# Mixing stage of a four-layer model: whole k and r products, state multiplies on GpSimd, another order of the steps

## The chip, the cores and the metric

The kernel runs on one core of a Trainium2 chip. A core has TensorE (matrix products), VectorE and ScalarE (elementwise work and activations), GpSimd (elementwise work as well) and SyncE, whose queue issues most DMA transfers. On-chip memory has 128 partitions; matrix products land in eight banks of a second memory, each 128 x 512 float32. Time is device microseconds of one execution, and lower is better.

## The reference

The model has four layers, each an attention-like part plus an expert part on a layer-normed input of 4 x 1024 tokens by 128 features. The change is in the first part of the last layer, and the last layer's 64 small experts run in the same stage.

```python
shifted = pad(x, one token)[:, :T];  delta = shifted - x
low = tanh((x + delta * mu_x) @ W_x1).reshape(B, T, 5, 32)
mus = einsum('blnr,dnr->blnd', low, W_x2) + x_bias
xr, xw, xk, xv, xg = [x + delta * mus[:, :, i] for i in range(5)]
r, k = xr @ W_r, xk @ W_k                      # 16 heads x 4
w = -exp(tanh(xw @ W_w1) @ W_w2 + b_w2)        # 16 heads x 4
v = xv @ W_v;  g = xg @ W_g                    # 16 heads x 8
def step(S, (r_t, k_t, v_t, w_t)):             # S: 4 x 8 per head
    o_t = r_t . S + (r_t * u * k_t).sum() * v_t
    S = exp(w_t) * S + outer(k_t, v_t)
o = group_norm(o) * gn_w + gn_b, times g * sigmoid(g), then @ W_o

# beside it: 64 experts and a shared one, 64 wide, top 8 of the router
out = sum_e gate_e * (silu(x @ Wg_e) * (x @ Wu_e)) @ Wd_e
```

## The kernel before

Everything lies transposed: features on the 128 partitions, the 4096 tokens along the row, cut into 8 chunks of 512 (`CH`, `BANK`). The last stage is `mixing_and_experts` (line 1739). It is written as a list of slots. From slot 12 on each slot holds one expert step: two experts, one chunk of tokens; 264 steps in all, 11 units of weights of 24 steps. The step goes through the engines with fixed lags. In slot t TensorE computes the hidden and the upper product (three float16 products each, from a high and a low part); ScalarE does silu in slot t; VectorE multiplies by the gate (`acted`, line 2298) and by the upper product (`scaled`, line 2304) in slot t+1; ScalarE makes the float16 high part in slot t+2 (line 2146); GpSimd makes the low part (`lows`, line 2185) in slot t+3; TensorE's output product stands in slot t+4. Every third step the sum is full: VectorE adds it to the result (line 2208) and TensorE may begin the next sum, in one bank, only after that.

The mixing lies between the steps. A chunk of it takes 33 slots (`PERIOD`), and the tables `PE_AT`, `ACT_AT`, `DVE_AT` and `POOL_AT` say in which slot of the chunk an engine does which job; a job of slot 37 falls into slot 4 of the next chunk. On each engine the order is: the expert step's work of the slot, then the mixing jobs, then on TensorE the output product. All waits are on counters of jobs done, so an engine that waits holds all that is queued behind it.

- TensorE's mixing products are float32 of 512 columns and take turns in two banks, `work`. A product waits until the reader of the last but one before it is done (`wait_bank`).
- Low-rank mixing factors: `low`, `low5`, `mu0` to `mu4`, then `mixed` (VectorE) and `x0` to `x4` (GpSimd) make the five inputs. `tanh_w`, `w` and two Exp on ScalarE (`ew`, `decay`) make the decay of 64 key rows, in `keys`. The Exp and the Sqrt each need a table load, and silu another one behind them.
- SyncE writes `keys` to DRAM (slot 10) and reads them back (slot 11) so that each row stands on the 8 partitions of its head's values: `rep`, 4 groups, one for each of a head's 4 keys. This read is called the spread here. SyncE also loads the gate rows, 6 transfers of 256 KB for every six steps into one of two buffers (line 1914), issued when the buffer's last reader is done, and the weights of the next unit (0.59 MB, line 1932).
- The state: for each group j TensorE computes the spread k (`k0` to `k3`) and r (`r0` to `r3`) with weights that repeat the columns; VectorE does `kv` (k times v), the `scan` along the tokens, `u` (adds u times kv to the state) and `rs` (times r); TensorE sums the four groups into `o_ps` (`o0` to `o3`), with the group mean taken off. Then `sq`, `var`, `std` (Sqrt), `rstd`, `norm`, `affine`, `gated`, and the product `out`, which VectorE adds to the result (`res`).

```python
banked = [job for job in pe_no if job[0] not in ("o0", "o1", "o2", "o3")]
bank_of = {job: i % 2 for i, job in enumerate(banked)}
bank_user = {job: banked[i - 2] for i, job in enumerate(banked) if i >= 2}
```

## Time and profile before

| | us |
|---|---|
| median of 3 runs | 4496.72 (4495.04 to 4506.08) |
| profiled execution | 4475.59 |
| its span, first to last instruction | 4473.8 |
| TensorE busy in the span | 3975.3 (89%) |
| VectorE busy | 3385.5 (76%) |
| ScalarE busy | 2913.3 (65%) |
| GpSimd busy | 2240.4 (50%) |

The expert steps of the last stage begin at 3744 us of the span. The shares of the table are means over all stages; for the change only the last one counts. A matmul's end in the trace is modelled: in a row of matmuls the starts tell the pace.

### The profile page before, as it was taken

Reading aid. Unit: us, or ns where it says so; the run is one execution under the profiler, and the core shown is the slowest. Engines: PE = TensorE matmul, PEld = TensorE weight load, DVE = VectorE, ACT = ScalarE, POOL = GpSimd, SP = SyncE. Lnnn points to the kernel's source line nnn. Section 1 sums busy time; section 2 is a strip of 40 time slices with the busy share of each in tenths; the row PEclk is TensorE's granted clock in tenths of the full one; section 3 lists DMA queues with packets and bytes.
Section 4 is the critical chain, followed back from the end, with each engine's and each line's share of the span. In section 5 each row is a group of like instructions: output and inputs, shape, how many; then the busy total and the mean of one; then the engine's idle time right before and its main releaser. Section 6 shows DMA issues by size and latency. Waiting matters only on the chain. (4 is left out here: it accounts for less than half of the span.)

```text
span 4473.8 us, 88017 instructions
## 1 busy us (share of the span) xinstructions
PE 3975.3 (89%) x34586; PEld 2227.3 (50%) x34588; DVE 3385.5 (76%) x4741; ACT 2913.3 (65%) x4403; POOL 2240.4 (50%) x1443
## 2 busy tenths in 40 slices
PE   6999999999999979996877777899788877999999
PEld 3666667666666654442111211245677543444443
DVE  6888888888884547767898899565877657878887
ACT  3777777777776449982677777685556644555555
POOL 2888888888886013331121210172566554555555
PEclk7999999999999989996899999898899988999999
DMA  3212212212210011100121100142000224454544
GB/s 84 59 40 59 58 38 59 59 40 58 58 35 16 1 49 48 71 24 29 50 74 43 40 27 16 57 149 72 11 13 15 75 83 115 113 124 116 120 113 108
DMA packets 113913, 270.28 MB, mean 60 GB/s; under 512 B 24276, under 2 KB 36308, under 8 KB 111004
## 3 DMA queue, kind: packets, MB, share of 16 engines
q1 hardware_dynamic: 98084, 223.86, 18.7%
q0 software_dynamic: 15424, 40.89, 2.6%
q8 instruction: 270, 4.42, 0.4%
q14 instruction: 135, 1.11, 0.1%
HBM read 178.10 MB, written 50.81 MB: 51 GB/s over the span
## 5 line engine op out<-in xcount | busy, mean ns | idle before, releaser
L522 POOL TENSOR_TENSOR a_prob_low<-a_prob_whole,a_prob_high 128x1024 f16<-128x1024 f32 x512 | 1085.0, 2131 | 276.7 <-ACT a_prob_high L412 275.6
L496 DVE TENSOR_REDUCE a_part_max<-a_top 128x2 f32<-128x1024 f32 x512 | 626.2, 1223 | 218.7 <-PE a_top L323 212.6
L409 ACT ACTIVATE a_prob_whole<-a_score 128x1024 f32<-128x1024 f32 x512 | 525.2, 1026 | 332.5 <-PE a_score L312 320.5
L976 ACT ACTIVATE a_prob<-a_score 128x512 f32<-128x512 f32 x1024 | 533.1, 603 | 255.9 <-PE a_score L915 255.8
L1009 DVE TENSOR_REDUCE a_part_max<-a_side 128x2 f32<-128x1024 f32 x512 | 595.2, 1220 | 68.3 <-PE a_side L886 68.3
L412 ACT ACTIVATE a_prob_high<-a_score 128x1024 f16<-128x1024 f32 x512 | 521.8, 1019 | 0.0
L311 PE MATMUL a_score<-a_qa,a_ka 128*128 128x256 f16 x2048 | 476.8, 273 | 0.0
L312 PE MATMUL a_score<-a_qb,a_kb 128*128 128x256 f16 x2048 | 476.5, 273 | 0.0
L2185 POOL TENSOR_TENSOR m_lows<-m_scaled,m_high 128x512 f16<-128x512 f32 x264 | 311.2, 1183 | 323.8 <-ACT m_high L2146 322.2
L378 PE MATMUL a_o_ps<-a_v,a_prob_high 128*128 128x65 f16 x4096 | 428.2, 193 | 6.2 <-POOL a_prob_low L522 3.4
L380 PE MATMUL a_o_ps<-a_v,a_prob_high 128*128 128x64 f16 x4096 | 427.0, 194 | 0.0
L382 PE MATMUL a_o_ps<-a_v,a_prob_low 128*128 128x65 f16 x4096 | 424.6, 192 | 0.0
L378 PEld LDWEIGHTS a_o_ps<-a_v,a_prob_high 128*128 128x128 f16 x4096 | 376.0, 96 | 85.7 <-DVE a_tokens L482 35.3
L380 PEld LDWEIGHTS a_o_ps<-a_v,a_prob_high 128*128 128x128 f16 x4096 | 377.8, 97 | 26.9 <-issue 10.9
L382 PEld LDWEIGHTS a_o_ps<-a_v,a_prob_low 128*128 128x128 f16 x4096 | 378.0, 98 | 0.0
L2138 ACT ACTIVATE m_up_down<-m_up_down 128x512 f32<-128x512 f32 x264 | 153.9, 583 | 341.4 <-PE m_up_down L1975 341.0
L915 PE MATMUL a_score<-a_qa,a_ka 32*128 32x512 f16 x1024 | 238.1, 399 | 90.6 <-ACT a_prob L976 88.0
L927 PE MATMUL a_o_ps<-a_prob,a_v 128*32 128x512 f32 x2048 | 287.6, 636 | 13.8 <-ACT a_raw L963 13.7
L915 PEld LDWEIGHTS a_score<-a_qa,a_ka 32*128 32x128 f16 x1024 | 60.4, 92 | 432.3 <-ACT a_prob L976 367.4
L2521 DVE TENSOR_TENSOR e_low<-e_whole,e_high 128x512 f16<-128x512 f32 x256 | 211.0, 834 | 83.9 <-ACT e_high L2479 82.9
L886 PE MATMUL a_side<-a_ka,a_qa 32*128 32x512 f16 x1024 | 218.1, 402 | 40.1 <-DVE a_part_max L1009 32.3
L2298 DVE TENSOR_TENSOR m_acted<-m_up_down,m_gate 128x512 f32<-128x512 f32 x264 | 180.4, 683 | 95.3 <-ACT m_up_down L2138 89.6
(477 smaller groups left out, 10147.8 us busy)
## 6 DMA issues: line engine op xcount, KB each, us to landing
m_gate<-gates SPq DMA_DIRECT2D x264, 256.0 KB, 5.2
a_ka<-a_nat_high_k SPq DMA_DIRECT2D x128, 128.0 KB, 2.4
e_gate<-gates SPq DMA_DIRECT2D x8, 2048.0 KB, 7.2
slots<-in_slots SPq DMA_DIRECT2D x19, 520.0 KB, 4.2
a_qa<-a_nat_high_q SPq DMA_DIRECT2D x64, 128.0 KB, 2.4
a_qa<-a_nat_low_q SPq DMA_DIRECT2D x64, 128.0 KB, 2.4
a_qb<-a_nat_high_q SPq DMA_DIRECT2D x64, 128.0 KB, 2.4
a_kb<-a_nat_low_k SPq DMA_DIRECT2D x64, 128.0 KB, 2.4
```

Source lines behind the costliest of these rows:

```text
L311: eng.matmul(score[:, e % 2, h, i, :], ka[:, r, h, keys], qa[:, r, h, qs], start=True, stop=False)
L312: mm = eng.matmul(score[:, e % 2, h, i, :], kb[:, r, h, keys], qb[:, r, h, qs], start=False, stop=True)
L378: eng.matmul(o_ps[:, at:at + V1], high, v[:, r, kt, h, 0:V1], start=(pair == 0 and i == 0 and h == 0 and t == 0), stop=False, skip_group_c ...
L380: eng.matmul(o_ps[:, at:at + DH], high, v[:, r, kt, h, V1 + 1:VW], start=False, stop=False, skip_group_check=True)
L382: mm = eng.matmul(o_ps[:, at:at + V1], low, v[:, r, kt, h, 0:V1], start=False, stop=last, skip_group_check=True)
L409: eng.activation(prob_whole[:, e % RING, :, :, :], score[:, e % 2, :, :, :], ACT.Exp, scale=scale)
L412: eng.activation(prob_high[:, e % RING, :, :, :], score[:, e % 2, :, :, :], ACT.Exp, scale=scale).then_inc(exp_done, 1)
L496: eng.tensor_reduce(part_max[:, i, c, :, qt % 4], top[:, :, :], AX.X, ALU.max).then_inc(max_done, 1)
L522: eng.tensor_tensor(prob_low[:, e % RING, :, :, :], prob_whole[:, e % RING, :, :, :], prob_high[:, e % RING, :, :, :], ALU.subtract).then_ ...
L976: eng.activation(prob[:, e % RING, h, :], score[:, step % SLOTS, :], ACT.Exp).then_inc(exp_done, 1)
L1009: op = eng.tensor_reduce(part_max[:, qt // 4, c, 2 * pair:2 * pair + 2, 24 + qt], side, AX.X, ALU.max)
L2185: eng.tensor_tensor(lows[:, s % HR, :], scaled[:, s % SR, :], high[:, s % HR, :], ALU.subtract).then_inc(low_done, 1)
```

## The change

The products for k and r are computed once for the 64 keys (`w_k` and `w_r` narrow, jobs `k` and `r`), and ScalarE copies them beside the decay into `keys`, now 64 x 3 x 512 (`kc`, `rc`). The write to DRAM and the spread carry all three, three times the bytes, in slots 12 and 13 instead of 10 and 11. GpSimd multiplies the spread k by v in place, two groups at a time (`kv01`, `kv23`, 128 x 1024), VectorE scans, GpSimd multiplies the spread r by the state in place (`rs01`, `rs23`), and TensorE takes that as operand of `o0` to `o3`. The direct term leaves the groups: VectorE makes r times u times k for 64 rows (`ruk`, into `z`), TensorE sums and spreads it over a head's values with 0/1 weights (`bonus`), VectorE multiplies by v (`av`), and TensorE adds that as a fifth product into `o_ps` (`oa`). The four `u`, four `kv` and four `rs` of VectorE are gone.

The tables change with it: the products `k`, `r`, `v`, `g`, `bonus` stand in slots 9 to 13, the outputs in 30 to 34, and what follows them (`var`, Sqrt, `norm`, `out`, `res`) six slots later than before, so in slots 3 to 11 of the next chunk. The sequence of the two banks changes with the sequence of the products.

```diff
-             "w": 8, "v": 9, "g": 11, "k0": 15, "r0": 16, "k1": 18, "r1": 19, "o0": 20, "k2": 21, "r2": 22, "o1": 23,
-             "k3": 24, "r3": 25, "o2": 26, "o3": 28, "var": 30, "out": 37}
+             "w": 8, "k": 9, "r": 10, "v": 11, "g": 12, "bonus": 13, "o0": 30, "o1": 31, "o2": 32, "o3": 33, "oa": 34,
+             "var": 36, "out": 43}
...
-    KEEP_AT, SPREAD_AT = 10, 11
+    KEEP_AT, SPREAD_AT = 12, 13
...
-        IN_ACT = {"low": "low", "low5": "low5", "tanh_w": "wt", "w": "ew", "v": "vs", "g": "gs", "var": "std"}
+        IN_ACT = {"low": "low", "low5": "low5", "tanh_w": "wt", "w": "ew", "k": "kc", "r": "rc", "v": "vs", "g": "gs", "var": "std"}
...
-                        after_act(eng, "decay", c)
-                        eng.dma_start(keys_d[:, :], keys[:, :]).then_inc(keys_out, 16)
+                        after_act(eng, "rc", c)
+                        eng.dma_start(keys_d[:, :], keys[:, :, :]).then_inc(keys_out, 16)
...
-                        eng.dma_start(rep[:, :, :], keys_d.rearrange("(h k) t -> h k t", k=GROUPS).unsqueeze(1).broadcast_to([16, 8, GROUPS, BANK])).then_inc(rep_in, 16)
+                        eng.dma_start(rep[:, :, :], keys_d.rearrange("(h k) t -> h k t", k=GROUPS).unsqueeze(1).broadcast_to([16, 8, GROUPS, 3 * BANK])).then_inc(rep_in, 16)
...
-                        after_dve(eng, f"rs{j}", c)
-                        eng.matmul(o_ps[:, :], const["center"][:, :], rs[:, j % 2, :], start=j == 0, stop=j == GROUPS - 1).then_inc(pe_done, 1)
+                        if name == "oa":
+                            after_dve(eng, "av", c)
+                        else:
+                            after_pool(eng, "rs01" if j < 2 else "rs23", c)
+                        eng.matmul(o_ps[:, :], const["center"][:, :], av[:, :] if name == "oa" else rep[:, j, W_R * BANK:(W_R + 1) * BANK],
+                                   start=name == "o0", stop=name == "oa").then_inc(pe_done, 1)
...
+                    elif name == "kc":
+                        after_pe(eng, "k", c)
+                        after_dve(eng, "ruk", c - 1)
+                        if c:
+                            eng.wait_ge(keys_out, 16 * c)
+                        op = eng.activation(keys[:, W_K, :], work[0:KEYS, bank_of["k", c], :], ACT.Copy)
...
+                    elif name[0:2] == "kv":
+                        two, own = slice(int(name[2]), int(name[3]) + 1), slice(W_K * BANK, (W_K + 1) * BANK)
+                        eng.wait_ge(rep_in, 16 * (c + 1))
+                        after_act(eng, "vs", c)
+                        op = eng.tensor_tensor(rep[:, two, own], rep[:, two, own], vs[:, :].unsqueeze(1).broadcast_to([P, 2, BANK]), ALU.mult)
+                    elif name[0:2] == "rs":
+                        two, own = slice(int(name[2]), int(name[3]) + 1), slice(W_R * BANK, (W_R + 1) * BANK)
+                        after_dve(eng, f"scan{name[3]}", c)
+                        op = eng.tensor_tensor(rep[:, two, own], rep[:, two, own], st[:, two, 0:BANK], ALU.mult)
...
                     elif name[0:4] == "scan":
-                        eng.wait_ge(rep_in, 16 * (c + 1))
-                        after_dve(eng, f"kv{j}", c)
-                        op = eng.tensor_tensor_scan(st[:, j, 1:BANK + 1], rep[:, j, :], kv[:, :], st[:, j, 0:1], ALU.mult, ALU.add)
+                        after_pool(eng, "kv01" if j < 2 else "kv23", c)
+                        after_dve(eng, "carry", c)
+                        op = eng.tensor_tensor_scan(st[:, j, 1:BANK + 1], rep[:, j, W_DECAY * BANK:(W_DECAY + 1) * BANK], rep[:, j, W_K * BANK:(W_K + 1) * BANK], st[:, j, 0:1], ALU.mult, ALU.add)
```

ScalarE before, slots 9 to 11 of a chunk (m_up_down is silu, m_high the high part, L2098 and L2101 the two Exp, m_vs the copy of v):

```order
L2138 ACTIVATE m_up_down<-m_up_down 128x512
L2146 ACTIVATE m_high<-m_scaled 128x512
L2098 ACT_TABLE_LOAD
L2098 ACTIVATE m_keys<-m_work,m_cols 64x512
L2101 ACTIVATE m_keys<-m_keys 64x512
L2138 ACT_TABLE_LOAD
L2138 ACTIVATE m_up_down<-m_up_down 128x512
L2146 ACTIVATE m_high<-m_scaled 128x512
L2093 ACTIVATE m_vs<-m_work 128x512
L2138 ACTIVATE m_up_down<-m_up_down 128x512
L2146 ACTIVATE m_high<-m_scaled 128x512
L2138 ACTIVATE m_up_down<-m_up_down 128x512
```

ScalarE after, the same slots (L2114 is the copy of k, L2120 that of r):

```order
L2157 ACTIVATE m_up_down<-m_up_down 128x512
L2165 ACTIVATE m_high<-m_scaled 128x512
L2105 ACT_TABLE_LOAD
L2105 ACTIVATE m_keys<-m_work,m_cols 64x512
L2108 ACTIVATE m_keys<-m_keys 64x512
L2157 ACT_TABLE_LOAD
L2157 ACTIVATE m_up_down<-m_up_down 128x512
L2165 ACTIVATE m_high<-m_scaled 128x512
L2114 ACTIVATE m_keys<-m_work 64x512
L2157 ACTIVATE m_up_down<-m_up_down 128x512
L2165 ACTIVATE m_high<-m_scaled 128x512
L2120 ACTIVATE m_keys<-m_work 64x512
```

The copy of k stands where the copy of v stood, behind both table loads, and the copy of r one slot later.

TensorE before, slot 8 from its mixing product `w` to slot 9's product `v`:

```order
L2039 MATMUL m_work<-m_wt,m_w_w 128x512
L1973 MATMUL m_out<-m_high,m_w_high 128x512
L1974 MATMUL m_out<-m_lows,m_w_high 128x512
L1975 MATMUL m_out<-m_high,m_w_low 128x512
L1973 MATMUL m_up_down<-m_x_high,m_w_high 128x512
L1974 MATMUL m_up_down<-m_x_low,m_w_high 128x512
L1975 MATMUL m_up_down<-m_x_high,m_w_low 128x512
L1973 MATMUL m_up_down<-m_x_high,m_w_high 128x512
L1974 MATMUL m_up_down<-m_x_low,m_w_high 128x512
L1975 MATMUL m_up_down<-m_x_high,m_w_low 128x512
L2042 MATMUL m_work<-m_mixed,m_w_v 128x512
```

TensorE after, slot 9 from its mixing product `k` to the two of slot 10, the `out` of the chunk before (m_cen) and `r`:

```order
L2051 MATMUL m_work<-m_mixed,m_w_k 128x512
L1972 MATMUL m_out<-m_high,m_w_high 128x512
L1973 MATMUL m_out<-m_lows,m_w_high 128x512
L1974 MATMUL m_out<-m_high,m_w_low 128x512
L1972 MATMUL m_up_down<-m_x_high,m_w_high 128x512
L1973 MATMUL m_up_down<-m_x_low,m_w_high 128x512
L1974 MATMUL m_up_down<-m_x_high,m_w_low 128x512
L1972 MATMUL m_up_down<-m_x_high,m_w_high 128x512
L1973 MATMUL m_up_down<-m_x_low,m_w_high 128x512
L1974 MATMUL m_up_down<-m_x_high,m_w_low 128x512
L2042 MATMUL m_work<-m_cen,m_w_o 128x512
L2054 MATMUL m_work<-m_mixed,m_w_r 128x512
```

Slot 10 now holds two mixing products; with `out` between them `k` and `r` use the same bank.

GpSimd before, from the last input of the second chunk (m_mixed) to the `delta` of the next:

```order
L2170 TENSOR_TENSOR m_mixed<-m_mixed,all_xn_t 128x512
L2185 TENSOR_TENSOR m_lows<-m_scaled,m_high 128x512 x4
L2154 TENSOR_TENSOR m_w_low<-m_w,m_w_high 128x1152
L2185 TENSOR_TENSOR m_lows<-m_scaled,m_high 128x512 x19
L2165 TENSOR_TENSOR m_delta<-m_zero,all_xn_t 128x1
L2166 TENSOR_TENSOR m_delta<-all_xn_t 128x511
```

GpSimd after, the same stretch from behind the weights' low part on (L2190 is k times v, L2194 r times the state):

```order
L2213 TENSOR_TENSOR m_lows<-m_scaled,m_high 128x512 x12
L2190 TENSOR_TENSOR m_rep<-m_rep,m_vs 128x2x512
L2213 TENSOR_TENSOR m_lows<-m_scaled,m_high 128x512
L2190 TENSOR_TENSOR m_rep<-m_rep,m_vs 128x2x512
L2213 TENSOR_TENSOR m_lows<-m_scaled,m_high 128x512 x3
L2194 TENSOR_TENSOR m_rep<-m_rep,m_st 128x2x512
L2213 TENSOR_TENSOR m_lows<-m_scaled,m_high 128x512 x2
L2194 TENSOR_TENSOR m_rep<-m_rep,m_st 128x2x512
L2213 TENSOR_TENSOR m_lows<-m_scaled,m_high 128x512
L2184 TENSOR_TENSOR m_delta<-m_zero,all_xn_t 128x1
L2185 TENSOR_TENSOR m_delta<-all_xn_t 128x511
```

From behind the twelfth of the nineteen `lows` on, four multiplies of 2 x 512 columns now stand between them.

## Rows read from the trace of the kernel before

**Rows 1.** Busy us of each engine (x count), granted clock, DMA share, GB/s; one chunk.
```profile
4016.00:4107.00 91.00, 86.84 (x348) 37.95 (x347) 75.08 (x106) 49.19 (x83) 51.51 (x42) 1.00 0.49 118
```

**Rows 2.** Timeline of TensorE: start us, us, line, operation [idle before <-releaser].
```profile
4021.74 0.38 PE L1973 MATMUL m_up_down<-m_x_high,m_w_high 128*128 128x512 f16 x1
...
4023.68 0.38 PE L1973 MATMUL m_up_down<-m_x_high,m_w_high 128*128 128x512 f16 x1
...
4024.98 1.02 PE L2045 MATMUL m_work<-m_mixed,m_w_k 128*128 128x512 f32 x2
...
4025.84 0.38 PE L1973 MATMUL m_out<-m_high,m_w_high 128*128 128x512 f16 x1
```

**Rows 3.** Timeline of ScalarE around Exp of two neighbouring chunks.
```profile
4010.11 0.58 ACT L2138 ACTIVATE m_up_down<-m_up_down 128x512 f32<-128x512 f32 x1 [1.68 <-PE m_up_down L1975]
...
4012.54 0.68 ACT L2098 ACTIVATE m_keys<-m_work,m_cols 64x512 f32<-64x512 f32 x1
...
4015.20 0.58 ACT L2138 ACTIVATE m_up_down<-m_up_down 128x512 f32<-128x512 f32 x1
...
4016.21 0.59 ACT L2093 ACTIVATE m_vs<-m_work 128x512 f32<-128x512 f32 x1
...
4103.68 0.68 ACT L2098 ACTIVATE m_keys<-m_work,m_cols 64x512 f32<-64x512 f32 x1
```

**Rows 4.** Timeline of ScalarE at the Sqrt.
```profile
4068.79 0.58 ACT L2138 ACTIVATE m_up_down<-m_up_down 128x512 f32<-128x512 f32 x1 [1.69 <-PE m_up_down L1975]
...
4071.22 0.69 ACT L2108 ACTIVATE m_std<-m_work,m_cols 128x512 f32<-128x512 f32 x1
```

**Rows 5.** Timeline of TensorE in the last chunk, where no mixing matmul stands.
```profile
4444.50 0.39 PE L1973 MATMUL m_out<-m_high,m_w_high 128*128 128x512 f16 x1 [2.76 <-DVE all_res_t L2208]
...
4457.43 0.39 PE L1973 MATMUL m_out<-m_high,m_w_high 128*128 128x512 f16 x1 [0.24 <-DVE all_res_t L2208]
```

**Rows 6.** Timeline of VectorE in the chunk of rows 2.
```profile
4020.35 0.68 DVE L2208 TENSOR_TENSOR all_res_t<-all_res_t,m_out 128x512 f32<-128x512 f32 x1
...
4020.95 0.68 DVE L2298 TENSOR_TENSOR m_acted<-m_up_down,m_gate 128x512 f32<-128x512 f32 x1
...
4021.72 0.69 DVE L2304 TENSOR_TENSOR m_scaled<-m_acted,m_up_down 128x512 f32<-128x512 f32 x1
...
4023.20 0.69 DVE L2298 TENSOR_TENSOR m_acted<-m_up_down,m_gate 128x512 f32<-128x512 f32 x1 [0.71 <-ACT m_up_down L2138]
...
4028.08 1.28 DVE L2256 TENSOR_TENSOR_SCAN m_st<-m_rep,m_st,m_kv 128x512 f32<-128x512 f32 x1
...
4036.37 1.71 DVE L2256 TENSOR_TENSOR_SCAN m_st<-m_rep,m_st,m_kv 128x512 f32<-128x512 f32 x1
```

**Rows 7.** Timeline of GpSimd in the same chunk.
```profile
4023.78 1.16 POOL L2185 TENSOR_TENSOR m_lows<-m_scaled,m_high 128x512 f16<-128x512 f32 x1 [1.84 <-ACT m_high L2146]
...
4028.53 1.79 POOL L2185 TENSOR_TENSOR m_lows<-m_scaled,m_high 128x512 f16<-128x512 f32 x1 [1.64 <-ACT m_high L2146]
...
4035.84 4.30 POOL L2185 TENSOR_TENSOR m_lows<-m_scaled,m_high 128x512 f16<-128x512 f32 x3
```

**Rows 8.** Groups of GpSimd, expert steps: line, xcount | busy us, mean ns | idle.
```profile
L2170 POOL TENSOR_TENSOR m_mixed<-m_mixed,all_xn_t 128x512 f32<-128x512 f32 x35 | 44.5, 1270 | 18.8 <-DVE m_mixed L2240 18.8
...
L2161 POOL TENSOR_TENSOR m_delta<-all_xn_t 128x512 f32<-128x512 f32 x4 | 4.2, 1042 | 0.0
```

**Rows 9.** Timeline of GpSimd ahead of the expert steps.
```profile
3732.28 2.13 POOL L2179 TENSOR_TENSOR m_x_low<-all_xn_t,m_x_high 128x1024 f16<-128x1024 f32 x1 [4.17 <-ACT m_x_high L2134]
```

**Rows 10.** Timeline of SyncE's queue: issues of keys and spread.
```profile
4105.09 0.47 SPq L1940 DMA_DIRECT2D keys<-m_keys  x1
...
4107.40 0.54 SPq L1945 DMA_DIRECT2D m_rep<-keys  x1
```

**Rows 11.** Two stretches with transfers under way; columns as in rows 1.
```profile
4108.50:4120.40 11.90, 11.00 (x48) 4.83 (x47) 9.58 (x15) 6.44 (x12) 6.64 (x7) 1.00 1.01 221
...
4020.00:4033.20 13.20, 12.33 (x52) 5.57 (x52) 11.36 (x18) 7.13 (x13) 6.27 (x6) 1.00 1.00 242
```

More of the change, by code:

```diff
@@ L2030, in mix @@
                         mm = eng.matmul(dst, const["w_g"][:, :], mixed[:, 4, :], start=True, stop=True)
+                    elif name == "bonus":
+                        after_dve(eng, "ruk", c)
+                        mm = eng.matmul(dst, const["bonus"][:, :], z[:, :], start=True, stop=True)
                     elif name == "var":
```

103 lines of the change are left out of this document (52 added, 51 removed).

## The prediction

> **What bounds the kernel now.** The change touches one stage, the last: expert steps with the mixing laid between them. I read the busy times of one chunk's stretch first, then the order of TensorE, then what ends its waits. In a chunk TensorE is busy 86.84 of 91.00 us, VectorE 75, GpSimd 52, and the granted clock is full, the 2.4 GHz level [rows 1]. So TensorE bounds the stage, and a microsecond counts where it lies on TensorE or makes TensorE wait.
>
> The price of a slot: two neighbouring slots without a mixing matmul start 1.94 us apart; a float32 matmul takes 0.86 us, from the start of a k product to what follows it [rows 2]. A chunk has 33 slots and 25 float32 matmuls: 33 x 1.94 = 64.0 and 25 x 0.86 = 21.5, together 85.5 us. From the Exp of one chunk to that of the next are 91.1 us [rows 3]. So TensorE waits 5.6 us a chunk, 45 us in 8 chunks.
>
> **What the change takes away.** Per chunk TensorE loses 8 products for k and r by group and gets 2 whole ones, the bonus product and the fifth into the outputs' bank: 25 becomes 21, 82.1 us instead of 85.5. Over 8 chunks that is 32 x 0.86 = 27.5 us, all of it on the engine that bounds. VectorE loses twelve operations of a chunk (kv, u, rs) and gets two; that is worth at most the 45 us of waits, which I take away whole and replace by those below. ScalarE's two extra copies lie beside TensorE's work, except where (b) counts them. Fewer constants arrive before the stage (one DMA more, less data): nothing, since the products of the first slots wait for other steps too.
>
> **What it adds.** Slots are those of a chunk; times in a slot count from the start of TensorE's expert products. A silu starts 0.85 us into the slot: acted follows it and starts 1.46 us after the products (4021.74 to 4023.20), a silu being 0.6 long [rows 2, 3, 6].
>
> (a) Slot 4: mu2 now takes the bank that var used, so it waits for the Sqrt of the chunk before, which ScalarE does in the same slot 4 behind silu, high and a table load. Sqrt ends 4071.22 + 0.69 - 4068.79 = 3.1 us after that silu [rows 4], so 4.0 into the slot; mu2 would start 6 x 0.216 = 1.3 into it. TensorE waits 2.7 us, with the expert steps behind it in its queue. Seven chunks have it: 18.9.
>
> (b) Slot 10: r takes the bank of k (the old out sits between them), so it waits for the copy of k, in ScalarE's slot 10 behind both table loads and both Exp. In the place of that copy stands vs today: it ends 4016.21 + 0.59 - 4010.11 = 6.7 us after the silu of slot 9 [rows 3], 7.5 after the start of slot 9. r would start at 2.80 + 1.29 + 0.86 = 4.95. Wait 2.6 us, seven times (the first chunk's mixing runs ahead of the steps): 18.2.
>
> (c) Slots 14 to 29 no longer hold a mixing matmul. In such slots TensorE catches up with VectorE's addition to the result every third step: today 0.24 shown as idle, and 0.16 by which a matmul's modelled end overlaps the next, 0.4 in all [rows 5]. Slots 16, 19, 22, 25: 1.6 a chunk, 12.8.
>
> (d) Slots 24 to 31. GpSimd gets four multiplies of 128x1024, VectorE's four scans stand in four slots running. No row shows the multiply. Bounds: twice 1.04 (delta) and twice 1.27 (mixed) [rows 8]; an existing one of 1024 columns takes 2.13 [rows 9]. I take 2.3, between the two that write float32. Scans and GpSimd's operations do not run beside each other: lows takes 1.79 instead of 1.16 when it starts within a scan, and a scan takes 1.71 instead of 1.28 when it starts within lows [rows 6, 7]. By hand, from the start of slot 24, with lows 1.1 and scan 1.2 in a row: lows to 1.2, multiply to 3.5, lows to 4.6, scan 0 to 5.8, multiply to 8.1, scan 1 to 9.3, lows to 10.4, lows to 11.5 (it is ready before scan 2, wanted at 10.7), scan 2 to 12.7. Then acted and scaled (0.77 + 0.61) and the addition 0.68 [rows 6]: the result is free at 14.8. TensorE's slot 28 would need it at 4 x 1.94 + 1.3 + 0.4 = 9.5: it waits 5.3. Scan 3 waits behind the next multiply to 17.3, and the products of slot 30 wait 0.6 more for acted. 5.9 a chunk: 47.2. The new waits of the outputs are met: the first wants its multiply at 19.3, and it is done at 16.1. With multiplies of 2.54 it is some 0.7 a chunk more; if scans could run beside GpSimd, 2.8.
>
> The Trainium skill, "SBUF — State Buffer", section "SBUF: two separate sides", speaks against the change: the port pair of VectorE and GpSimd is an exclusive lock held for a whole instruction by a GpSimd operation or a VectorE one with two SBUF inputs. The overlaps in rows 6 and 7 agree; for the long multiplies no run yet shows it. By the rule (d) is 47, without it 22.
>
> (e) Transfers. The spread grows from 1.05 to 3.15 MB, the keys from 0.13 to 0.39. The next gate rows (1.57 MB, six steps) are issued by SyncE behind the spread. Today a spread and gate rows, 2.62 MB, fill the stretch 4108.5 to 4120.4 at 221 GB/s, another stretch runs at 242, the DMA engines' share at 1.0 in both [rows 11]; I take 230, and that the queue is served in order. From the end of the copy of r: the spread is issued 2.3 us after the keys today [rows 10], 3.5 with the longer keys, and its bytes start 1.1 later, at 4.7. In odd chunks gate rows follow it: (3.15 + 1.57) / 0.23 = 20.5, in at 25.2. VectorE needs them in slot 22: 3 x 2.80 + 7 x 1.94 + 0.8 from slot 11, 1.46 into the slot, less 2.45, where the copy of r ends (0.85, then 1.0 of silu and high, then 0.6 [rows 3]): 21.8. Wait 3.4. In even chunks gate rows precede and follow: 1.6 + (0.39 + 1.57 + 3.15 + 1.57) / 0.23 = 30.6, needed in slot 25 at 28.0. Wait 2.6. The first chunk starts with its gates loaded. 4 x 3.4 + 3 x 2.6 = 21.4, and 5 for two chunks where a weight load (0.59 MB, 2.6 us) stands ahead too: 26.4. At 242 it is some 8 less, at 221 some 7 more. Moving keys and spread two slots later costs nothing by itself: the multiplies want the spread in slot 24, after it is in. On SyncE the keys now wait for the copy of r, with spread, weight loads and gate rows behind them; that is in these times.
>
> (f) The last chunk's Sqrt stays in slots without mixing, as today (2.76 of idle [rows 5]): 3.
>
> **Sum.** 18.9 + 18.2 + 12.8 + 47.2 + 26.4 + 3 = 126.5 of new waits, less 45 of old ones, less 27.5 of products: +54. The profiled execution takes 4475.6 us, 1.8 more than its span; with the change 4530. It lies 21.1 under the median of the runs shown, 4496.7; the same addition makes the median **4551**.
>
> **Rivals.**
> The gate rows land in time, because the queue moves more than 230 GB/s or is not served in order. Then (e) goes: +28, 4525. For it: no wait for a gate row is seen today. Against: the share of 1.0. The Trainium skill, "DMA: Bandwidth & Descriptors", section "Anatomy of one DMA — SWDGE (gpsimd) path", has 2.0 us plus bytes over 436 GB/s; this rival is what it would give, its estimate for the spread is 9.2 us, and rows 11 do not agree.
> The port is not exclusive for the new operations: (d) is 22, the sum +29, 4526.
> Faster: TensorE's own work bounds slots 14 to 32. If VectorE, relieved of twelve operations, keeps up there, and gates and scans hide behind its slack, (c), (d) and (e) are gone: 54 - 86 = -32, 4465. It decides faster or not from 54 us gained in these slots. Against: the scans in four slots running need 1.2 each on an engine whose slot already holds 1.38 + 0.2 of 1.94.
> Worse: a late weight load makes ScalarE wait as well, or the waits delay each other: some 90, 4587.
>
> **How the numbers follow.** Forecast 0.60, gates in time 0.13, port shared 0.10, faster 0.09, worse 0.08. Within 0.3% (13.5 us, about what a measurement of this kernel can tell from no change) would need two of the rivals at once, or the faster one in part: by the low ends of (d) and (e) together, -25 and -26, +3 is left; I give it 0.08 out of the forecast's share. So faster 0.09, same 0.08, slower 0.83. The range starts at +10, near both low ends of (d) and (e). It goes to +80: multiplies of 2.54 (+6), 221 GB/s (+7), GpSimd's weight splits that fall into slots 24 to 27 of two chunks (2.4 each), and some delay between the waits. 4507 to 4577.
>
> **What would show it.** TensorE: 21 float32 matmuls a chunk; about 2.7 of idle before mu2 in slot 4, released by ScalarE's Sqrt, and 2.6 before r, released by the copy of k. VectorE: scans longer than 1.28 in most chunks, as long as GpSimd's operation before them; multiplies of 2.1 to 2.5. VectorE's acted in slot 22 or 25 released by a DMA. A chunk's period near 98 us instead of 91.1. Wrong would be: a period under 91, no idle before r or mu2, or gate rows that land ahead of the step that uses them.

## The result, and the profile after

The change makes the kernel slower: 4607.8 us against 4501.4 (medians of four runs each), a ratio of 1.0233, interval 1.022 to 1.0246. That is 106 us; the forecast was 54, at most 80. The direction held, the size did not.

The whole difference lies in the last stage. Chunks are counted from 0. From the Exp of chunk 0 (the first after the stage's lead-in) to the end are 846.6 us in the profiled execution after, 736.5 before. The stages ahead are untouched, and they happen to have taken some 18 to 38 us less in the profiled execution of before than in all the others; so I compare this length of the stage, and the medians beside it.

ScalarE's Exp in two neighbouring chunks of the changed kernel, as [rows 3] show it before (start us, duration, line, operation):

```profile
3868.34 0.68 ACT L2105 ACTIVATE m_keys<-m_work,m_cols 64x512 f32<-64x512 f32 x1
...
3974.58 0.68 ACT L2105 ACTIVATE m_keys<-m_work,m_cols 64x512 f32<-64x512 f32 x1
```

One chunk takes 106.2 us here, where it was 91.1. The other full periods are 98.8 to 110.1. The two chunks as windows (columns as in [rows 1]; the third row is a stretch that is spoken of below):

```profile
3868.34:3974.58 106.24, 89.19 (x341) 37.24 (x340) 70.89 (x96) 50.52 (x84) 63.07 (x46) 0.94 0.54 124
3974.58:4073.42 98.84, 86.12 (x341) 36.58 (x340) 68.98 (x96) 49.54 (x83) 59.02 (x44) 0.97 0.55 126
3909.60:3913.40 3.80, 3.79 (x9) 1.31 (x10) 1.72 (x4) 1.02 (x2) 0.00 (x0) 0.50 0.76 173
```

TensorE's busy time is not what it was for the same products: 341 of them instead of 348 [rows 1], and yet 86 to 89 us. The granted clock is 0.94 and 0.97 instead of 1.00. The third window shows why: 9 products in 3.8 us at a granted clock of 0.50, which is the lower of the two levels, 1.2 GHz. So there are two things to read on TensorE's timeline: the waits, and the pace behind them.

TensorE at mu2 and at r in chunk 2 (start us, duration, line, operation, in brackets the idle time before and who ended it):

```profile
3953.87 0.38 PE L1974 MATMUL m_up_down<-m_x_high,m_w_low 128*128 128x512 f16 x1
3956.80 1.16 PE L2027 MATMUL m_work<-m_low,m_w_x 128*128 128x512 f32 x2 [2.56 <-ACT m_std L2127]
3957.77 0.62 PE L1972 MATMUL m_out<-m_high,m_w_high 128*128 128x512 f16 x1
3958.18 0.63 PE L1973 MATMUL m_out<-m_lows,m_w_high 128*128 128x512 f16 x1
...
3960.74 0.60 PE L1973 MATMUL m_up_down<-m_x_low,m_w_high 128*128 128x512 f16 x1
3961.17 0.39 PE L1974 MATMUL m_up_down<-m_x_high,m_w_low 128*128 128x512 f16 x1
...
3975.40 1.04 PE L2042 MATMUL m_work<-m_cen,m_w_o 128*128 128x512 f32 x2
3978.88 1.12 PE L2054 MATMUL m_work<-m_mixed,m_w_r 128*128 128x512 f32 x2 [2.44 <-ACT m_keys L2114]
3979.84 0.38 PE L1972 MATMUL m_out<-m_high,m_w_high 128*128 128x512 f16 x1
```

mu2 (L2027) waits 2.56 us for the Sqrt and r (L2054) 2.44 us for the copy of k, as forecast. (The modelled end of a matmul overlaps the next; by the distance of starts it is 2.7 and 2.6.) New is what follows mu2: the float16 products start 0.43 us apart instead of 0.216, from 3957.77 to 3961.17. Behind this r the pace is the full one; behind three of the seven r it is not.

TensorE behind the wait for gate rows in chunk 1:

```profile
3909.61 0.61 PE L1972 MATMUL m_out<-m_high,m_w_high 128*128 128x512 f16 x1 [7.61 <-DVE all_res_t L2236]
3910.01 0.63 PE L1973 MATMUL m_out<-m_lows,m_w_high 128*128 128x512 f16 x1
...
3913.00 0.58 PE L1974 MATMUL m_up_down<-m_x_high,m_w_low 128*128 128x512 f16 x1
3913.41 0.38 PE L1972 MATMUL m_out<-m_high,m_w_high 128*128 128x512 f16 x1
```

This wait was forecast as 3.4 us and is 7.61, and nine products behind it run at half pace.

What ended the waits of the stage (in sum, times, longest), of the changed kernel; PEld, the weight load of a product, waits with it:

```profile
DVE m_acted L2322 <- DMA m_gate<-gates: 43.2, 6, 8.6
...
PEld m_work L2054 <- ACT m_keys L2114: 22.9, 7, 3.3
PEld m_work L2027 <- ACT m_std L2127: 21.3, 7, 3.1
ACT m_w_high L2076 <- DMA m_w<-in_w_small: 18.5, 2, 10.9
```

VectorE waits six times for gate rows, and ScalarE twice for weights, up to 10.9 us: the eight chunks have one such wait each. I have followed all starts of TensorE's products through the stage and put each distance beyond the pace of an instruction (0.216 us, 0.86 for a whole float32 one) down either to a wait, where the next instruction shows idle time, or to the lower pace, where it shows none. That gives this account of the stage, in us:

| term | forecast | measured |
|---|---|---|
| (a) mu2 behind the Sqrt | 18.9 | 19.0 |
| (b) r behind the copy of k | 18.2 | 18.3 |
| (c) slots without mixing, 0.34 to 0.47 each | 12.8 | 9.7 |
| (d) slots with multiplies and scans | 47.2 | 30.0 |
| (e) gate rows and weights | 26.4 | 62.1 |
| (f) the end | 3 | 5.2 |
| all waits after | 126.5 | 144.4 |
| waits of before that go | -45 | -46.2 |
| products at full pace (32 fewer of 0.86) | -27.5 | -27.5 |
| first wait of the stage, for an input (3.1 after, 4.4 before) | none | -1.3 |
| lower pace (45.7 after, 4.8 before) | none | +40.9 |
| sum | +54 | +110 |

The last line agrees with the difference of the stages (110.1). Some 3 us of either number for the lower pace are short distances of 0.1 to 0.4 us at the full clock; they cancel. So the forecast lacks a term of 41 us, and (e) is short by 36 while (d) is 17 too long.

### The profile page after: what moved, and what is told of

Its sections match the earlier page's. It is cut to its first block and busy times, and to the rows that moved or that the text cites. A ratio compares the mean times of both kernels' runs of the same rounds, so it can differ in the third digit from the quotient of the medians.

```text
span 4610.0 us, 87772 instructions
## 1 busy us (share of the span) xinstructions
PE 3996.8 (87%) x34524; PEld 2224.5 (48%) x34524; DVE 3348.7 (73%) x4661; ACT 2918.3 (63%) x4419; POOL 2321.3 (50%) x1475
## 5 line engine op out<-in xcount | busy, mean ns | idle before, releaser
L2213 POOL TENSOR_TENSOR m_lows<-m_scaled,m_high 128x512 f16<-128x512 f32 x264 | 323.6, 1229 | 323.7 <-ACT m_high L2165 323.2
L380 PEld LDWEIGHTS a_o_ps<-a_v,a_prob_high 128*128 128x128 f16 x4096 | 377.7, 97 | 26.9 <-issue 10.9
```

What stands on the lines that cost most here:

```text
L380: eng.matmul(o_ps[:, at:at + DH], high, v[:, r, kt, h, V1 + 1:VW], start=False, stop=False, skip_group_check=True)
L2213: eng.tensor_tensor(lows[:, s % HR, :], scaled[:, s % SR, :], high[:, s % HR, :], ALU.subtract).then_inc(low_done, 1)
```

## Experiments

Theory after this reading: the waits are the forecast's with other sizes, (d) and (e) cover each other, and TensorE falls to its lower clock because it stood idle. Rivals: the lower clock comes from something else in the change; the queue as a whole is overloaded; what is taken away comes back as another wait. Each run was compared with the kernel before in the same place; the median of before was 4500 to 4506 there. In the table, "stage" is the length from the first Exp to the end, "waits" and "pace" are the account above; the first wait of the stage, 2.9 to 4.6 us in every run, is left out of "waits". The diffs below are shortened, and their comments are added to the code.

| run | median us | ratio to before | stage | waits | pace |
|---|---|---|---|---|---|
| before | 4501.4 | 1 | 736.5 | 46 | 5 |
| changed | 4607.8 | 1.022 to 1.0246 | 846.6 | 144 | 46 |
| 1 bank waits away | 4567.6 | 1.0093 to 1.0187 | 793.5 | 103 | 32 |
| 2 spread in halves | 4575.6 | 1.0138 to 1.0192 | 813.2 | 116 | 39 |
| 3 multiplies and scans apart | 4585.1 | 1.0162 to 1.0215 | 820.0 | 131 | 33 |
| 4 waits filled | 4606.7 | 1.021 to 1.0278 | 840.7 | 100 | 32 |
| 5 three gate buffers | 4561.7 | 1.0086 to 1.0153 | 798.5 | 105 | 37 |
| 6 before, more spread | 4535.1 | 1.0041 to 1.008 | 771.2 | 72 | 14 |
| 7 all at once | 4505.2 | 0.999 to 1.0013 | 736.0 | 59 | 19 |
| 8 before, addition first | 4487.9 | 0.9949 to 0.9977 | 720.1 | 26 | 8 |
| 9 all at once, mended | 4476.2 | 0.9934 to 0.996 | 709.3 | 37 | 13 |
| 10 no multiplies, on run 5 | 4550.6 | 1.008 to 1.0112 | 779.8 | 91 | 30 |
| 11 changed, addition first | 4594.4 | 1.0182 to 1.0214 | 826.0 | 133 | 34 |
| 12 one idle wait, on run 8 | 4527.6 | 1.0038 to 1.0065 | 763.1 | 60 | 18 |
| 13 the same wait filled | 4522.4 | 1.0025 to 1.0054 | 755.5 | 34 | 9 |

**Run 1, (a) and (b) alone.**
```diff
-    "kc": 10, ... "sq": 35, "std": 37,
+    "kc": 9,  ... "sq": 35, "std": 36,
```


> The changed kernel with ScalarE's Sqrt one slot earlier (36 instead of 37) and the copy of k one slot earlier (9 instead of 10), so that mu2 finds its bank free and r finds the copy done. In the changed kernel mu2 waits 2.7 us seven times and r 2.6 us seven times, 37.3 us in all, and TensorE runs 45.7 us longer than its instructions need at full pace, in stretches that follow such waits. Theory A (the forecast's waits, and on top of them a clock that falls after a wait): the 37 us go and with them a part of the 45.7, since a chunk loses 5.7 us of pace and only about 1.9 of them stand behind the gate wait: 45 to 60 us less, 4548 to 4563. Theory B (only the waits cost; the lower clock belongs to something else): 35 to 37 us less, 4571 to 4573. Theory C (the waits hide others, which come out when these go): under 25 us less, above 4583.

40 us less by the medians (its runs spread from 4541 to 4578), 53 by the stage. Both waits are gone from the trace, 37 us, and 14 of the lower pace with them. The other waits are 103 in place of 107: those behind gate rows and weights are 10 shorter, and one small wait came out, of the product v, 1.1 us seven times, for VectorE to read the bank of `out`. Theory A by the stage; by the medians the gain lies between A and B.

**Run 2, the spread in halves.**
```diff
-    KEEP_AT, SPREAD_AT = 12, 13
+    KEEP_AT, SPREAD_AT = 12, (13, 18)   # groups 0, 1 and groups 2, 3, a semaphore each
```


> The changed kernel with the spread issued in two halves, groups 0 and 1 in slot 13, groups 2 and 3 in slot 18, so that the gate rows no longer stand behind 3.15 MB. In the changed kernel VectorE and ScalarE wait for gate rows or weights in slot 22 or 25 of each chunk and TensorE waits 5.7 to 11.5 us behind them, 62 us in 8 chunks; the waits of the slots with scans and multiplies are 30 us, less than the 47 forecast. Theory A (gate rows late behind the spread, and the burst in part hidden behind that wait): the 62 go, 17 of the burst come out, 10 to 20 of the lower clock's 45.7 go as well: 50 to 65 us less, 4543 to 4558. Theory B (the queue's whole load is what is late, so another group of gate rows waits as long): 0 to 25 us less. Theory C (gate waits alone, burst not hidden): 75 us less, 4533.

32 us less: between A and B. In odd chunks TensorE's wait in slot 22 falls from 7.5 to 11.5 us to 0.8 to 3.2. In even chunks it stays at 5.8 to 6.8, because there gate rows are issued in slot 19 and still have both halves ahead of them. In chunk 5 ScalarE waited 5.4 us for weights instead, and TensorE 6.0 behind it. The edit moved the place in the queue for half the chunks only.

**Run 3, the burst drawn apart.**
```diff
-    "scan0": 25, "scan1": 26, "scan2": 27, "scan3": 28,   "kv01": 24, "kv23": 25, "rs01": 28, "rs23": 30
+    "scan0": 24, "scan1": 26, "scan2": 28, "scan3": 29,   "kv01": 23, "kv23": 25, "rs01": 27, "rs23": 30
```


> The changed kernel with the state multiplies and scans drawn apart: multiplies in slots 23, 25, 27 and 30 instead of 24, 25, 28 and 30, scans in 24, 26, 28 and 29 instead of 25 to 28. TensorE's waits behind that stretch are 30 us in 8 chunks, 24 of them in chunks 1, 3, 5 and 7 and the first. Theory A (GpSimd and VectorE exclude each other, so four scans in a row beside four multiplies hold up lows and the result's addition): 10 to 20 us less, 4588 to 4598. Theory B (their sum, not their order, is what is too long): within 5 us of the changed kernel.

23 us less, a little more than A: waits behind these slots go from 30 to 18, and 13 of pace come back.

**Run 4, work put into the waits.**
```diff
+    if at < CH and at and here == 10: filler(slot, 10)
     for name, c in pe_jobs[slot]: mix(name, c)
+    if at < CH and at and here == (22 if at % 2 else 25): filler(slot, 24)
+    # filler: float16 products of 512 columns into o_ps
```


> The changed kernel with work added to TensorE: in chunks 1 to 7, 10 float16 products of 512 columns ahead of r in slot 10, and 24 ahead of the out products in slot 22 (odd chunks) or 25 (even chunks). They write the outputs' bank while nothing of use stands in it and are overwritten. At 0.216 us each they take 2.2 and 5.2 us, and TensorE waits 2.6 and 5.7 to 11.5 us there anyway. Theory A (TensorE's clock falls to the lower level because it stood idle): the waits stay filled, the stretch of nine products at 0.43 us behind the gate wait runs at 0.216, and 10 to 20 us are gained although 51 us of products were added: 4588 to 4598. Theory B (the lower clock has another cause): no gain, 0 to 10 us more where a filler reaches past its wait.

The same time with 51 us more of products. The lower pace falls from 45.7 to 32.2 us, and behind the seven filled waits for k no product runs slowly any more (three did). Behind the gate rows slow products stay, 1.4 to 1.7 us lost, wherever 2.5 us of waiting or more are left. But the gain was not kept: what TensorE gains between the copy of r and slot 22 or 25 it waits for gate rows there, since their landing counts from that copy; and in chunk 3 the wait comes earlier, for weights, so that the filler (5.2 us) lay on the path. The clock's part is supported, not yet isolated; runs 12 and 13 do that.

**Run 5, gate rows issued earlier.**
```diff
-    gate = pl.sb("gate", [P, 2, J, PAIR])   # issued 6 slots ahead
+    gate = pl.sb("gate", [P, 3, J, PAIR])   # issued 12 slots ahead; HR 6 -> 4 for the room
```


> The changed kernel with three buffers of gate rows instead of two (and four of high and lows instead of six, to make room), so that gate rows are issued 12 slots ahead instead of 6, and with the spread issued ahead of gate rows of the same slot. 12 slots are 23 us; spread and gate rows, 4.72 MB, take 21 us at the 222 GB/s that the changed kernel's trace shows. Theory A (the rows are late because they stand behind the spread, and the wait hides a part of the burst): the waits of 5.7 to 11.5 us go, 62 in all, the burst comes out at its forecast 47 instead of 30, and of the 45.7 of lower clock 10 to 20 go: 55 to 65 us less than the changed kernel, 4543 to 4553. Theory B (the queue as a whole is overloaded): another group of rows waits instead, under 20 less. Theory C (the burst was sized right by itself but the wait does not hide it): 72 to 82 less.

46 us less by the medians, 48 by the stage, short of A's 55. Of the gate waits of chunks 1 to 7, 1.0 to 2.5 us on VectorE are left in three; in the first chunk TensorE still waits 7.9 for weights. What was behind them comes out, if less than A said: the waits behind scans and multiplies are 39 us in 8 chunks instead of 30, and the increase is in the even chunks, 4.0 to 6.5 instead of 0.9 to 1.4. TensorE in chunk 1 of this run, behind lows and behind the addition:

```profile
3914.34 0.39 PE L1975 MATMUL m_out<-m_high,m_w_high 128*128 128x512 f16 x1 [2.00 <-POOL m_lows L2216]
...
3918.49 0.39 PE L1975 MATMUL m_out<-m_high,m_w_high 128*128 128x512 f16 x1 [2.04 <-DVE all_res_t L2239]
```

**Run 6, the transfer alone, in the kernel before.**
```diff
     eng.dma_start(rep[:, :, :], keys_d ... broadcast).then_inc(rep_in, 16)
+    for i in range(2):
+        eng.dma_start(more[:, i * GROUPS:(i + 1) * GROUPS, :], keys_d ... broadcast).then_inc(more_in, 16)
```


> The kernel before with the transfer of the change alone: behind each spread of 1.05 MB two more of 1.05 MB into a tile that nothing reads. No multiply, copy or product is changed. Its spread goes out two slots, 3.9 us, earlier than in the changed kernel, whose waits behind gate rows and weights are 62 us. Theory A (bytes ahead of the gate rows make VectorE wait, and the clock falls behind that): 62 less 8 x 3.9 = 31 us of waits and up to 2 us of lower clock for each, 25 to 47 us more than before, 4525 to 4547, and a granted clock that leaves the full level in this stage, where before it never does. Theory B (the forecast's bytes and rate: its waits of 3.4 and 2.6 us vanish with 3.9 us of head start): within 5 us of before, clock at the full level.

29 us more than before: A. VectorE's acted in chunk 2, and TensorE behind it:

```profile
3986.67 0.69 DVE L2304 TENSOR_TENSOR m_acted<-m_up_down,m_gate 128x512 f32<-128x512 f32 x1 [7.11 <-DMA m_gate<-gates]
```

```profile
3988.79 0.61 PE L1979 MATMUL m_out<-m_high,m_w_high 128*128 128x512 f16 x1 [6.37 <-DVE all_res_t L2214]
3989.19 0.63 PE L1980 MATMUL m_out<-m_lows,m_w_high 128*128 128x512 f16 x1
...
3991.75 0.49 PE L1980 MATMUL m_up_down<-m_x_low,m_w_high 128*128 128x512 f16 x1
3992.07 0.38 PE L1981 MATMUL m_up_down<-m_x_high,m_w_low 128*128 128x512 f16 x1
```

A kernel without the state multiplies on GpSimd waits 7.11 us for gate rows, its TensorE 6.37, and its next eight products start 0.43 apart. Its other waits of this kind are 5.5 and 1.6 us on TensorE behind gate rows, 6.2 and 12.2 behind weights; the lower pace follows all but the one of 1.6.

**Run 7, all suspected waits at once.** The edits of runs 1 and 5, both halves of the spread in slots 13 and 14, multiplies and scans between slots 19 and 29, and VectorE's addition ahead of acted:
```diff
+    add_to_res(...)          # of step LAG + 1
     acted; scaled
-    add_to_res(...)
```


> The changed kernel with every suspected wait taken away at once: Sqrt and copy of k one slot earlier; three buffers of gate rows; the spread in two halves in slots 13 and 14; multiplies in slots 19, 21, 24 and 29 and scans in 20, 22, 24 and 26; and VectorE's addition to the result ahead of acted in its slot instead of behind acted and scaled, where VectorE waits for the silu anyway. Theory A (the loss is these waits and the clock that follows them): the clock stays at the full level, the 27.5 us of removed products show, and the waits for the addition that the kernel before has (32 us) go too: 4500 - 27.5 - 32 = 4440, and up to 30 more where GpSimd and VectorE still exclude each other: 4440 to 4470, below before. Theory B (the stage of the changed kernel is bound by something that these edits leave, transfers or GpSimd's sum): 4500 to 4560.

103 us less than the changed kernel and level with before: the loss is these waits, but A's 4440 is missed. In even chunks the second half of the spread stood behind gate rows, and TensorE waited 5.6 to 6.7 us behind GpSimd.

**Run 8, the addition first, in the kernel before.** The last diff alone.

> The kernel before with one thing of the last run alone: VectorE's addition to the result ahead of acted in its slot. In the kernel before, TensorE waits 32 us of the stage for that addition. Theory A (it is late only because it stands behind acted and scaled): 25 to 32 us less than before, 4468 to 4475. Theory B (TensorE waits for VectorE's whole load, whatever its order): within 8 us of before.

18 us less than before, in a ratio of 0.9949 to 0.9977. The waits for the addition fall from 32 to 3 us, but of the waits ahead of mixing products 1.3 us a chunk stays and 0.8 is new; between A and B.

**Run 9, the mended combination.** Against run 7; the copies of v and g and the product `av` move one slot along.
```diff
-    SPREAD_AT = (13, 14); "scan0": 20, "scan1": 22, "scan2": 24, "scan3": 26; "kv23": 21, "rs01": 24, "rs23": 29
+    SPREAD_AT = (13, 13); "scan0": 20, "scan1": 23, "scan2": 26, "scan3": 29; "kv23": 24, "rs01": 25, "rs23": 30
-    "r": 10, "v": 11, "g": 12, "bonus": 13
+    "r": 11, "v": 12, "g": 13, "bonus": 14
```


> The run with every suspected wait taken away, mended where its trace still shows waits: its second half of the spread stood behind gate rows in even chunks, and GpSimd waited 5.6 to 6.7 us there (period 92 to 94 us, odd chunks 89.4 to 92); a scan takes 2.0 to 2.4 us beside GpSimd's operations and VectorE gains only some 0.4 us a slot back; r waited 1.1 us for the copy of k. So: both halves in slot 13 ahead of the gate rows, scans three slots apart (20, 23, 26, 29), multiplies in 19, 24, 25 and 30, r, v, g and the bonus product one slot later. Theory A (what was left are these waits): the period falls to 83 to 86 us where the instructions alone need 82.1, the granted clock stays at the full level, 4450 to 4475 us, below the kernel before and below the 4488 of the kernel before with its addition first. Theory B (GpSimd's and VectorE's sum is the bound): periods of 88 to 90 us, 4480 to 4500.

4476.2 us, 27.5 less than before in the same comparison: 0.5% faster than before, clear of noise, and by its median and its stage (709 against 720) faster than run 8, though the intervals of the two overlap. The wait of 1.1 us that the expectation gives to r was v's, the one of run 1. Two of its chunks:

```profile
3856.18:3942.23 86.05, 83.32 (x341) 36.13 (x340) 69.24 (x96) 50.35 (x85) 63.31 (x47) 1.00 0.68 158
3942.23:4028.89 86.66, 83.53 (x341) 36.05 (x340) 69.66 (x96) 49.48 (x83) 60.99 (x45) 1.00 0.65 147
```

Behind the first chunk the periods are 86.0 to 89.2 us, the clock at 1.00 in these two. A was 83 to 86 and 4450 to 4475 and is just missed; some 3.5 us a chunk of waits for lows and acted are left. That the stage is 27 us shorter than before is not the removed products alone, since the addition is first here. Run 8 has that too, and against it the stage is 11 us shorter: 27.5 of products less, 11 of waits and 5 of pace more.

**Run 10, without the multiplies.** Run 5 with each multiply cut to one column of each group; state and outputs are then not those of the reference.
```diff
-    op = eng.tensor_tensor(rep[:, two, own], rep[:, two, own], vs...broadcast_to([P, 2, BANK]), ALU.mult)
+    op = eng.tensor_tensor(rep[:, two, own][:, :, 0:1], rep[:, two, own][:, :, 0:1], vs[:, 0:1]..., ALU.mult)
```


> The run with three buffers of gate rows, with GpSimd's four multiplies of a chunk cut to one column of each group (1 instead of 512), so that the state and the outputs are computed without them; the price of the burst by itself, without gate waits to hide it. With the multiplies TensorE's waits behind slots 24 to 31 are 4.4 to 8 us a chunk in that run. Theory A (the forecast's (d): the multiplies, exclusive with the scans, hold up lows and the addition, 5.9 a chunk): 35 to 45 us less than 4562 and some 10 of lower clock, 4507 to 4520. Theory B (the four scans in a row hold up VectorE also without GpSimd's multiplies): under 20 us less, above 4542.

Only 11 us less than run 5 by the medians, whose intervals overlap, and 19 by the stage: B either way. The waits behind these slots go from 39 to 26 us. TensorE at the place of the last two rows of run 5, and the group of the scans in this run:

```profile
3924.94 0.39 PE L1975 MATMUL m_out<-m_high,m_w_high 128*128 128x512 f16 x1 [2.89 <-DVE all_res_t L2239]
```

```profile
L2292 DVE TENSOR_TENSOR_SCAN m_st<-m_rep,m_st 128x512 f32<-128x512 f32 x32 | 48.4, 1511 | 1.2 <-POOL m_rep L2193 1.2
```

Against 2.00 and 2.04 one wait of 2.89 for the addition remains. The scans take 1.51 us here instead of 2.12 in run 5, so they do lose time beside the multiplies; but four scans in four slots on an engine with 0.36 us to spare in each (1.94 less the prediction's 1.38 and 0.2) hold up the addition also alone.

**Run 11, the addition first, in the changed kernel.** The diff of run 8.

> The changed kernel with VectorE's addition to the result ahead of acted in its slot, and nothing else. The waits of 0.4 in the slots without a mixing product (forecast 12.8 us, in the changed kernel's trace about 10) go; those behind scans and multiplies go in part, since the addition no longer stands behind a held-up acted, but the ones of lows stay. Theory A: 10 to 25 us less than the changed kernel, 4583 to 4598. Theory B (the gate rows' landing sets the time from the copy of r to slot 22 or 25, and what is gained ahead of it is waited there): the gate waits grow by what the slots ahead of them gain, and the run is within 8 us of the changed kernel.

13 us less, A at its low end: the waits of (c) are gone, and most of the other waits are now ended by acted instead of the addition.

**Runs 12 and 13, the clock by itself.** Into run 8, whose clock is full in this stage from chunk 1 on, one wait is put in chunks 1 to 7, idle or filled:
```diff
+    # SyncE, slot 14 or 17: two transfers of 7 KB, the second issued when the first has landed
+    # TensorE, same slot, run 13 only: 18 float16 products of 512 columns into o_ps
+    eng.wait_ge(ping, 32 * c)
```


> The kernel before with its addition first (4488 us, clock at the full level in this stage, no wait over 3 us in full chunks), with one wait put into chunks 1 to 7, in slot 14 or 17: when TensorE has done a slot's first products, SyncE sends two short transfers of 7 KB, one after the other, into a tile that nothing reads, and TensorE goes on when they have landed. From the keys' transfer to the spread behind it 3.5 us pass in the changed kernel, most of it landing, so two should make TensorE wait 3.5 to 6 us, 25 to 42 us in all. Theory A (an idle TensorE loses its clock, and gets it back some us after it works again): on top of the waits 1.4 to 2.9 us behind each, 10 to 20 us. Theory B (the clock falls for another reason that the changed kernel has, its multiplies or its transfers): only the waits are added.

> The same kernel with the same waits, and 18 float16 products of 512 columns (3.9 us at 0.216) ahead of each, into the outputs' bank, which nothing uses in these slots. Theory A: no half-paced products behind the waits, 10 to 20 us less than the run with the waits idle, although TensorE has 27 us more of products. Theory B: the same time as with the waits idle, or more by what the products reach past the wait.

TensorE in chunk 1 with the wait idle, then filled:

```profile
3855.98 0.38 PE L1983 MATMUL m_up_down<-m_x_high,m_w_low 128*128 128x512 f16 x1
3862.03 0.61 PE L1981 MATMUL m_out<-m_high,m_w_high 128*128 128x512 f16 x1 [5.67 <-DMA m_scratch<-in_cols]
3862.43 0.63 PE L1982 MATMUL m_out<-m_lows,m_w_high 128*128 128x512 f16 x1
...
3865.85 1.91 PE L2053 MATMUL m_work<-m_mixed,m_w_k 128*128 128x512 f32 x2
3867.55 0.55 PE L1981 MATMUL m_out<-m_high,m_w_high 128*128 128x512 f16 x1
```

```profile
3857.78 4.05 PE L2069 MATMUL m_o_ps<-m_x_high,m_w_high 128*128 128x512 f16 x18
3864.06 0.39 PE L1981 MATMUL m_out<-m_high,m_w_high 128*128 128x512 f16 x1 [2.23 <-DMA m_scratch<-in_cols]
3864.29 0.38 PE L1982 MATMUL m_out<-m_lows,m_w_high 128*128 128x512 f16 x1
```

And two odd chunks of each, idle and filled (granted clock behind the busy times):

```profile
3846.54:3944.63 98.09, 90.36 (x349) 38.41 (x348) 74.06 (x106) 49.20 (x83) 50.19 (x42) 0.97 0.47 112
4036.20:4133.65 97.45, 88.57 (x349) 37.98 (x348) 73.36 (x106) 49.34 (x82) 47.92 (x41) 0.96 0.48 119
```

```profile
3848.13:3943.79 95.66, 91.36 (x367) 39.42 (x366) 74.07 (x106) 49.23 (x82) 50.28 (x42) 1.00 0.48 115
4035.81:4131.24 95.43, 91.02 (x367) 39.51 (x366) 73.37 (x106) 49.38 (x82) 47.96 (x41) 1.00 0.51 121
```

Idle, the wait is 5.67 us, and all up to 3867.55 behind it runs at half pace, the float32 product too (1.70 from start to start instead of 0.86). Filled, 2.23 are left of it, and the first product behind it has the full pace. Six of the seven idle waits, 3.4 to 7.2 us long, are followed by slow products, 10.8 us in all; of the filled ones one, whose rest was 2.85. With 126 products more (27 us of TensorE's time) these chunks are 2.0 to 2.4 us shorter. By the medians it is 5.2 us less and by the stage 7.6, under the 10 to 20 expected, as the even chunks lose at most 1.7 us to the clock and one gave back nothing. The intervals of the two runs overlap, so the times alone do not decide; the traces do. The granted clock of the stage is 0.97 idle and 0.99 filled, and in the account the 27 us of products take the place of 26 us of waits, so that the 9 us less at the lower pace are what the stage gains. Run 13 adds to run 12 nothing but work in TensorE's idle time, so the idling is the cause: theory A, with a smaller gain than it said.

## Why the forecast had the sign and not the size

**Products, (a), (b), (c).** Right, with (c) somewhat too long. 21 float32 matmuls a chunk; 19.0 and 18.3 us at mu2 and r against 18.9 and 18.2; run 1 takes both away. They could be worked out because both sides of each wait stand in the trace of before [rows 2 to 4]. (c) is 9.7 against 12.8 (run 11).

**(d).** The size by itself was not far off, 39 us where no gate wait hides it (run 5) against 47. Two steps were wrong. The sum added (d) to (e), but in even chunks the gate wait lies in slot 25, within the burst, and GpSimd works through its multiplies meanwhile: only 0.9 to 1.4 us are left there, 30 in all. And more than half of the term was put on the multiplies' exclusion (47 with it, 22 without); run 10, whose multiplies are one column wide, still waits 26, so the multiplies cost 13. That the two engines slow each other down is there. Groups of VectorE and GpSimd in the changed kernel (times, mean ns):

```profile
L2289 DVE TENSOR_TENSOR_SCAN m_st<-m_rep,m_st 128x512 f32<-128x512 f32 x32 | 62.9, 1966 | 3.3 <-POOL m_rep L2190 3.3
L2213 POOL TENSOR_TENSOR m_lows<-m_scaled,m_high 128x512 f16<-128x512 f32 x264 | 323.6, 1229 | 323.7 <-ACT m_high L2165 323.2
L2190 POOL TENSOR_TENSOR m_rep<-m_rep,m_vs 128x1024 f32<-128x1024 f32 x16 | 40.4, 2523 | 0.9 <-DMA m_rep<-keys 0.9
L2194 POOL TENSOR_TENSOR m_rep<-m_rep,m_st 128x1024 f32<-128x1024 f32 x16 | 34.8, 2175 | 0.0
```

Scans take 1.97 us on the mean, against 1.28 alone [rows 6], and the multiplies 2.52 and 2.18 where I took 2.3. Without the multiplies the scans take 1.51 (run 10).

**(e).** The term that was mis-sized most among those that the forecast names: 62 for 26, gate rows 42 for 21 and weights 20 for 5. In the last chunk the copy of r ends at 4505.1. SyncE's queue (start us, duration of the issue) and VectorE's acted in slot 22:

```profile
4505.21 0.47 SPq L1939 DMA_DIRECT2D keys<-m_keys  x1
4508.80 0.54 SPq L1944 DMA_DIRECT2D m_rep<-keys  x1
4514.06 16.10 SPq L1913 DMA_DIRECT2D m_gate<-gates  x12
```

```profile
4534.11 0.69 DVE L2322 TENSOR_TENSOR m_acted<-m_up_down,m_gate 128x512 f32<-128x512 f32 x1 [7.64 <-DMA m_gate<-gates]
```

```profile
4509.90:4534.10 24.20, 18.55 (x83) 7.77 (x81) 12.51 (x19) 10.89 (x20) 11.56 (x10) 0.94 1.00 214
```

The packets of the same stretch:

```profile
DMA packets 751, 5.19 MB, mean 214 GB/s; under 512 B 127, under 2 KB 127, under 8 KB 621
```

Keys and spread go out as forecast (3.6 us apart, 3.5 said). The gate rows are in 29.0 us after the copy instead of 25.2; they were wanted at 21.3 instead of 21.8. The queue moved 214 GB/s, not 230, and 5.2 MB instead of 4.72 in that stretch. The other 0.45 MB are the next six gate rows: the row with x12 holds two groups of six issues, the second from 4526.49 on, and of the packets 621 - 127 = 494 are gate rows of 4 KB, where six transfers of 256 KB are 384. So the 4.72 MB that VectorE waited for took 24.2 us, 195 GB/s. In chunk 2, an even one, it is 33.3 instead of 30.6, and 27.5 instead of 28.0. Both numbers are 2 to 15% off, and the wait is their difference: 7.6 instead of 3.4, 5.9 instead of 2.6. The weights were priced at 5 for two chunks. ScalarE's wait for them, at the one in chunk 3:

```profile
4094.82 0.58 ACT L2157 ACTIVATE m_up_down<-m_up_down 128x512 f32<-128x512 f32 x1 [1.24 <-PE m_up_down L1974]
4106.31 1.16 ACT L2076 ACTIVATE m_w_high<-m_w 128x1152 f16<-128x1152 f32 x1 [10.90 <-DMA m_w<-in_w_small]
```

The weights are issued right behind the spread:

```profile
4085.42 0.54 SPq L1944 DMA_DIRECT2D m_rep<-keys  x1
4086.01 0.58 SPq L1931 DMA_DIRECT2D m_w<-in_w_small  x1
```

The wait is 10.9 us, since they stand behind the whole spread: 20 us pass from their issue to ScalarE's start. On TensorE 11.5 us of waiting stand behind it and 8.2 behind the first chunk's (7.6 on ScalarE), 20 us together. That is the rival "worse", which got 0.08; its mechanism came true beside the forecast's.

**The clock.** The step that failed is the first: "the granted clock is full, the 2.4 GHz level", read off a chunk whose longest wait is 1.3 us, and then used for a kernel to which the same text gave waits of 2.6, 2.7, 3.4 and 5.3 us in each chunk. 41 us of the missing 56 (110 of the stage less 54) are this. Behind all eight gate and weight waits (5.7 to 11.5 us) the changed kernel runs at half pace for 3 to 6 us, 1.5 to 2.9 us lost each time; behind six of seven waits for mu2, and three of seven for r, it loses 1.6 to 1.8. Together these are 34 of the 45.7; most of the rest stands behind the waits of (d), the stage's first and its last. The Trainium skill, "TensorE: Matmul & The Clock Gate", section "HAM oscillation — how this bites in real kernels", says as much: work behind a wait for a transfer starts at the lower clock again, at every such wait; this trace agrees, with the 0.43 us at 3909.61. The forecast didn't weigh it.

**Range and rivals.** "Gates in time", "port shared" and "faster" did not happen. The formula that stands beside "gates in time" is, by its heading, one for transfers that GpSimd issues; SyncE issues these. The range ended at +80 since it widened each named term but none for a clock; with waits of the forecast's own sizes, some 1.7 us behind three long waits a chunk would have put 41 on its centre, as one sees afterwards.

## What to carry to other kernels

When an edit puts waits like these, of 2.6 us and more, on a TensorE whose waits had been short (up to 1.3 us in a full chunk here), add 1.5 to 2.9 us of half pace for most of them (17 of 22 here), and count waits that lie within one another once. A wait for a transfer is the difference of two long stretches: work out both to the microsecond, count the bytes that are still in the queue, and allow for a rate below the lowest that the trace shows (221 GB/s there, 214 here), or issue what is urgent earlier (run 5). An addition that an engine can do while it waits for another's result belongs ahead of that result.
